# Message sums of a graph layer in turns of 24 steps, with rows fetched by byte offsets into two places

## The reference, cut to what matters

```
h   = relu(x @ w1 + b1)
msg = ew[:, None] * h[src]
agg = segment_sum(msg, dst, num_segments=12500)
z   = agg @ w2 + b2
out = relu(batch_norm(z))        # and a second batch norm behind it
```

## Time and profile before

| what | us |
|---|---|
| median of 3 runs | 5294.92 |
| lowest and highest | 5294.16, 5295.47 |
| the profiled execution's own time | 5292.76 |
| its span, first to last instruction | 5290.7 |
| first gather of layer 1's sum to its last add | 190.86 to 2100.60 |
| first gather of layer 2's sum to its last add | 2260.84 to 4170.76 |

### The profile page before, as it was taken

How to read it: one execution, slowest core, us unless ns; L and a number is a source line. 1 busy time by engine, 2 the same in 40 slices (tenths; PEclk the granted TensorE clock), 3 DMA queues, 4 the chain that set the end, 5 groups by cost and what they waited for, 6 DMA issues and landing times. The chain is left out here.

```text
span 5290.7 us, 129431 instructions
## 1 busy us (share of the span) xinstructions
PE 4201.0 (79%) x20156; PEld 3563.5 (67%) x20157; DVE 3115.8 (59%) x8711; ACT 855.8 (16%) x1985; POOL 3822.4 (72%) x3848
## 2 busy tenths in 40 slices
PE   6778788787787877668777777888778488699998
PEld 5666666666666666556666666666666388599998
DVE  6555555555555555655555555555555665566665
ACT  4200000000000000500000000000000365454444
POOL 2577777777777776677777777777777367678887
PEclk9776767767767676876777777776776555799999
DMA  5433333333333333233333333333333287245554
GB/s 158 131 108 108 108 108 108 108 108 108 108 108 108 108 108 91 91 109 108 109 108 108 108 108 108 108 109 108 108 108 108 67 192 154 48 78 78 79 78 74
DMA packets 360681, 560.51 MB, mean 106 GB/s; under 512 B 128514, under 2 KB 254114, under 8 KB 360483
## 3 DMA queue, kind: packets, MB, share of 16 engines
q0 software_dynamic: 192864, 454.73, 33.0%
q1 hardware_dynamic: 134434, 85.69, 6.7%
q10 hardware_dynamic: 33312, 19.33, 1.4%
HBM read 478.91 MB, written 80.47 MB: 106 GB/s over the span
## 5 line engine op out<-in xcount | busy, mean ns | idle before, releaser
L836 POOL DMA_INDIRECT c_messages<-h,c_indices x3038 | 2880.7, 948 | 950.8 <-issue 919.3
L872 PE MATMUL c_partial<-c_onehot,c_messages 128*128 128x128 f32 x12544 | 2794.3, 375 | 811.8 <-DMA c_messages<-h,c_indices 411.0
L872 PEld LDWEIGHTS c_partial<-c_onehot,c_messages 128*128 128x128 f32 x12544 | 2289.5, 262 | 1319.1 <-issue 767.9
L915 DVE TENSOR_TENSOR sums<-sums,c_partial 128x256 f32 x3136 | 1322.3, 422 | 1591.0 <-PE c_partial L872 1534.4
L888 DVE TENSOR_SCALAR c_onehot<-iota,edge_dst,edge_w 128x128 f32<-128x128 f32 x3152 | 1152.0, 366 | 12.7 <-PEq L113 12.6
L798 ACT ACTIVATE c_indices<-edge_src 128x16 int32 (+1 forms) x200 | 42.9, 215 | 3706.3 <-PE c_partial L872 2914.8
L1804 POOL DMA_INDIRECT out<-ffn_result,ffn_table x210 | 335.0, 1595 | 88.7 <-issue 35.2
L1845 PE MATMUL ffn_ps<-ffn_xT,ffn_w_tile 128*128 128x256 f32 x1680 | 381.9, 381 | 0.0
L1845 PEld LDWEIGHTS ffn_ps<-ffn_xT,ffn_w_tile 128*128 128x128 f32 x1680 | 313.1, 191 | 37.8
L1787 POOL DMA_INDIRECT ffn_rows<-tokens,ffn_table x218 | 239.5, 1099 | 67.9 <-issue 62.2
L852 PE MATMUL c_z<-sums,w 128*128 x768 | 266.1, 510 | 0.0
(11 more groups left out here) (184 smaller groups left out, 2656.2 us busy)
## 6 DMA issues: line engine op xcount, KB each, us to landing
c_messages<-h SPq DMA_DIRECT2D x6272, 1.0 KB
c_messages<-h ACTq DMA_DIRECT2D x6272, 1.0 KB
c_messages<-h,c_indices POOLq DMA_INDIRECT x3038, 2.8
pi_x<-in_x SPq DMA_DIRECT2D x14, 896.0 KB
h<-pi_h ACTq DMA_DIRECT2D x14, 896.0 KB
rt_x<-in_x SPq DMA_DIRECT2D x14, 896.0 KB
out<-rt_x SPq DMA_DIRECT2D x14, 896.0 KB
tokens<-rt_tokens SPq DMA_DIRECT2D x14, 896.0 KB
```

What stands on the lines that cost most here:

```text
L836: pool.indirect_dma_start(messages[:, k, :], None, source, bass.IndirectOffsetOnAxis(ap=indices[:, k:k + 1], axis=0)).then_inc(s_message[k ...
L872: last = pe.matmul(partial[:, k % TURN_BANKS, g * P:(g + 1) * P], messages[:, k, g * P:(g + 1) * P], onehot[:, k % TURN_ONEHOTS, :], start ...
L915: dve.tensor_tensor(where, where, partial[:, k % TURN_BANKS, 0:C].rearrange("p (g n) -> p g n", g=CG), ALU.add).then_inc(s_added, 1)
```

## The change

A turn has 24 steps, not 32. There are 65 full turns and a short one of 3 steps, so all 1563 steps and no empty ones. POOL gathers 23 steps of a full turn and the 3 of the short one. The chunk of nodes per turn is 192, not 256, and there are 65 chunks; the product stands before step 16 and the statistics before step 20.

The fetched step has two slots (`place` 0 and 1), used in turn, so the loops of SP, ACT and PE hold two turns in a round. A turn's rows wait until the turn before the last has been multiplied. The sources are offsets in bytes: `plan_tiles` multiplies the fetched steps' row numbers by 1024 into `row_offset`, and each DMA takes a register as it is for the offset into the source seen as bytes. Registers are loaded 32 at a time, and the next column is fetched behind the second load. ACT no longer copies indices; DVE does, after steps 11 and 22. `add_bias` stands between two fetches of ACT.

```diff
-TURN = 32
+TURN = 24
 FETCHED = TURN - 1
-HALVES = ((0, 16), (16, FETCHED))
+HALVES = ((0, 12), (12, FETCHED))
 TURN_BANKS = 4
 TURN_ONEHOTS = 8
-TURNS = -(-EDGE_TILES // TURN)
+TURNS = EDGE_TILES // TURN
+STEPS_LEFT = EDGE_TILES - TURNS * TURN
-ROW_BATCH = 16
+ROW_BATCH = 32
+ROW_BYTES = C * 4
-Z_COLS = 256
+Z_COLS = 192
-Z_AT = 16
+Z_AT = 12
...
                 dve.tensor_copy(dest[:, c0 * P:c1 * P], turned[:, g % 4, 0:(c1 - c0) * P]).then_inc(s_out, 1)
+                if (a, c1) == (0, K):
+                    dve.wait_ge(s_out, g + 1)
+                    dve.tensor_scalar(t["row_offset"][:], t["edge_src"][:, FETCHED:FETCHED + TURNS * TURN + 1:TURN],
+                                      float(ROW_BYTES), None, ALU.mult)
...
-        messages = sb("messages", [P, TURN, C], F32)
+        messages = sb("messages", [P, TURN + 1, C], F32)
-        s_row = [sem("s_row_sp"), sem("s_row_act")]
+        s_row = [[sem(f"s_row_{e}{u}") for u in range(2)] for e in ("sp", "act")]
+        source_bytes = source.rearrange("(a n) c -> a (n c)", a=1).bitcast(U8)
...
                 eng.dma_start(row_index[0:1, b, :],
-                              t["edge_src"][b * SHARE:(b + 1) * SHARE, bass.ds(turn * TURN + FETCHED, 1)]
+                              t["row_offset"][b * SHARE:(b + 1) * SHARE, bass.ds(turn, 1)]
                               ).then_inc(s_column[b], 16)
-        def fetch_rows(eng, regs, b, turn):
+        def load_offsets(eng, regs, b, batch):
+            eng.load(regs, row_index[0:1, b, batch * ROW_BATCH:(batch + 1) * ROW_BATCH])
+        def fetch_batch(eng, regs, b, batch, place):
+            for n in range(ROW_BATCH):
+                first = bass.RuntimeValue.of_register_unchecked(regs[n]).with_bounds(
+                    min_val=0, max_val=(NODES_PAD - 1) * ROW_BYTES)
+                row = b * SHARE + batch * ROW_BATCH + n
+                eng.dma_start(messages[row:row + 1, FETCHED + place, :].bitcast(U8),
+                              source_bytes[0:1, bass.ds(first, ROW_BYTES)]).then_inc(s_row[b][place], 16)
+        def fetch_rows(eng, regs, b, turn, place):
             gate(eng, s_column[b], turn * 16 + 16, passed)
-            for first in range(0, SHARE, ROW_BATCH):
-                eng.load(regs, row_index[0:1, b, first:first + ROW_BATCH])
-                for n in range(ROW_BATCH):
-                    node = eng.snap(regs[n], min_val=0, max_val=NODES_PAD - 1)
-                    row = b * SHARE + first + n
-                    eng.dma_start(messages[row:row + 1, FETCHED, :], source[bass.ds(node, 1), :]
-                                  ).then_inc(s_row[b], 16)
+            load_offsets(eng, regs, b, 0)
+            if not isinstance(turn, int):
+                gate(eng, s_multiplied, turn * TURN, passed)
+            fetch_batch(eng, regs, b, 0, place)
+            load_offsets(eng, regs, b, 1)
             fetch_column(eng, b, turn + 1)
+            fetch_batch(eng, regs, b, 1, place)
...
             fetch_column(sp, 0, 0)
-            with sp.Fori(0, TURNS) as i:
-                gate(sp, s_multiplied, (i + 1) * TURN, passed)
-                fetch_rows(sp, regs, 0, i)
+            fetch_rows(sp, regs, 0, 0, 0)
+            with sp.Fori(0, TURNS // 2) as i:
+                fetch_rows(sp, regs, 0, i * 2 + 1, 1)
+                fetch_rows(sp, regs, 0, i * 2 + 2, 0)
...
-            turn_of(0, False)
-            with act.Fori(1, TURNS) as i:
-                turn_of(i, True)
+            fetch_rows(act, regs, 1, 0, 0)
+            with act.Fori(0, TURNS // 2) as i:
+                fetch_rows(act, regs, 1, i * 2 + 1, 1)
+                add_bias(i * 2)
+                fetch_rows(act, regs, 1, i * 2 + 2, 0)
+                add_bias(i * 2 + 1)
...
+            pool.wait_ge(s_index, TURNS * 2 + 1)
+            for k in range(STEPS_LEFT):
+                gather(k)
...
+                    slot = FETCHED + place if k == FETCHED else k
...
                         for b in range(2):
-                            pe.wait_ge(s_row[b], i * (16 * SHARE) + 16 * SHARE)
+                            pe.wait_ge(s_row[b][place], round_ * (16 * SHARE) + 16 * SHARE)
...
-            turn_of(0, False)
-            with pe.Fori(1, TURNS) as i:
-                turn_of(i, True)
+            turn_of(0, TURN, False)
+            with pe.Fori(0, TURNS // 2) as i:
+                turn_of(i * 2 + 1, TURN, True, 1, i)
+                turn_of(i * 2 + 2, TURN, True, 0, i + 1)
+            turn_of(TURNS, STEPS_LEFT, False)
...
+            def copy_indices(turn, half):
+                first, end = HALVES[half]
+                dve.tensor_copy(indices[:, first:end], t["edge_src"][:, bass.ds(turn * TURN + first, end - first)]
+                                ).then_inc(s_index, 1)
...
                     build(k % TURN_ONEHOTS, n + TURN_ONEHOTS).then_inc(s_onehot, 1)
+                    for half, (first, end) in enumerate(HALVES):
+                        if k == end - 1:
+                            copy_indices(i + 1, half)
...
+            t["row_offset"] = held("row_offset", [P, TURNS + 1], I32)
```

More of the change, by code:

```diff
@@ L21 @@
 U32 = mybir.dt.uint32
+U8 = mybir.dt.uint8
 P = 128
@@ L785, in _ @@
             fetch_column(sp, 0, 0)
-            with sp.Fori(0, TURNS) as i:
-                gate(sp, s_multiplied, (i + 1) * TURN, passed)
-                fetch_rows(sp, regs, 0, i)
+            fetch_rows(sp, regs, 0, 0, 0)
+            with sp.Fori(0, TURNS // 2) as i:
+                fetch_rows(sp, regs, 0, i * 2 + 1, 1)
+                fetch_rows(sp, regs, 0, i * 2 + 2, 0)
             sp.wait_ge(s_column[0], 16 * (TURNS + 1))
-            sp.wait_ge(s_added, TURN_BANKS + TURNS * TURN)
+            sp.wait_ge(s_added, TURN_BANKS + EDGE_TILES)
         @block.scalar
         def _(act):
-            def copy_indices(turn, first, end):
-                act.activation(indices[:, first:end], t["edge_src"][:, bass.ds(turn * TURN + first, end - first)],
-                               ACT.Copy).then_inc(s_index, 1)
             regs = [act.alloc_register(f"{name}_row{n}") for n in range(ROW_BATCH)]
-            for first, end in HALVES:
-                copy_indices(0, first, end)
             fetch_column(act, 1, 0)
@@ L811, in add_bias @@
                                    bias=t["columns"][:, 0, co:co + 1]).then_inc(s_z_biased, 1)
-            def turn_of(i, with_chunk):
-                gate(act, s_multiplied, (i + 1) * TURN, passed)
-                fetch_rows(act, regs, 1, i)
-                for first, end in HALVES:
-                    gate(act, s_multiplied, (i + 1) * TURN + end, passed)
-                    copy_indices(i + 1, first, end)
-                    if first == 0 and with_chunk:
-                        add_bias(i - 1)
-            turn_of(0, False)
-            with act.Fori(1, TURNS) as i:
-                turn_of(i, True)
+            fetch_rows(act, regs, 1, 0, 0)
[4 more added lines that the diff above has]
+                add_bias(i * 2 + 1)
             act.wait_ge(s_column[1], 16 * (TURNS + 1))
@@ L830, in _, with gather @@
         def _(pool):
+            def gather(k):
+                pool.indirect_dma_start(messages[:, k, :], None, source,
+                                        bass.IndirectOffsetOnAxis(ap=indices[:, k:k + 1], axis=0)
+                                        ).then_inc(s_message[k], 16)
             with pool.Fori(0, TURNS) as i:
@@ L835, in _ @@
                     for k in range(first, end):
-                        pool.indirect_dma_start(messages[:, k, :], None, source,
-                                                bass.IndirectOffsetOnAxis(ap=indices[:, k:k + 1], axis=0)
-                                                ).then_inc(s_message[k], 16)
+                        gather(k)
+            pool.wait_ge(s_index, TURNS * 2 + 1)
+            for k in range(STEPS_LEFT):
+                gather(k)
         @block.tensor
@@ L855, in product_of, with turn_of @@
                 last.then_inc(s_z, 1)
-            def turn_of(i, with_chunk):
-                for k in range(TURN):
+            def turn_of(i, steps, with_chunk, place=0, round_=0):
+                for k in range(steps):
                     n = i * TURN + k
+                    slot = FETCHED + place if k == FETCHED else k
                     if k == Z_PRODUCT and with_chunk:
@@ L917, in turn_of @@
                                       ALU.add).then_inc(s_added, 1)
+                    if steps < TURN:
+                        continue
                     build(k % TURN_ONEHOTS, n + TURN_ONEHOTS).then_inc(s_onehot, 1)
+                    for half, (first, end) in enumerate(HALVES):
+                        if k == end - 1:
+                            copy_indices(i + 1, half)
+            for half in range(len(HALVES)):
+                copy_indices(0, half)
             dve.sem_inc(s_added, TURN_BANKS)
```

20 lines of the change are left out of this document (12 added, 8 removed).

## The result

| | before | after |
|---|---|---|
| median of the runs, us | 5294.54 (5292.66 to 5295.47, 4 runs) | 5229.82 (5226.58 to 5235.25, 4 runs) |
| the profiled execution, us | 5292.76 | 5229.11 |
| its span, us | 5290.7 | 5227.4 |
| TensorE's mean granted clock | 0.744 | 0.766 |

The ratio is 0.9877, with a 95% interval of 0.9866 to 0.9889: faster by 64.7 us. The direction, the engine that sets the pace and the length of a turn came out as written; 12 us of gain were not in the sum. (On some chips the kernel before took about 8250 us; no time measured there is set beside one from the other chips.)

The account below looks back on a forecast made before the run. POOL's gathers were taken to bound the message sums. Gathers -50.2, ends -3.8, aggregation +1.7 and row_offset +0.5 summed to -51.8 us from 5292.76, so 5241.0; with 2.16 for the median, 5243, range 5236 to 5268.

Parts of the forecast that it names:

- the gathers' term: POOL's first to last gather: fewer gathered steps per layer, 25.1 us less per layer, 50.2 in all.
- the ends' term: Last gather to end of each layer's sums: z product seven steps earlier, 1.9 us less per layer, 3.8 in all.
- The pace maker: Message sums: POOL's gathers set the pace, a full turn of 23 gathers taking 28.84 us.
- SP's turn: SP's row fetches, loads and gates: 32.8 us a turn falls to 27.0, 1.8 under POOL's.
- the ceiling: SP's load of 32 registers: at most 3.6 us, from twice 74 ns for each of the added 16; 2.25 taken.
- rival A: SP's or ACT's fetch becomes the bound, through the 32-register load or the loop's way back; up to 5355 or 5393; 12%.
- Rival B: Row fetch: rows keep their register operation (SP's turn 32.4, 5706 us) or byte DMAs are cut up (7305); slower; 7%.
- ACT's chain: ACT's rows, behind add_bias: 27.0 us issuing plus up to 2.8 landing, at most 29.8 against 31.1 available.
- DVE and the aggregation: DVE: index copies and added statistics cost nothing; aggregating 65 chunks, not 49, adds 1.7 us over four times.
- TensorE: PE in the message sums: work stays about 1512 us in 1877, 81% busy.

Follow-up runs that it names:

- the operation put back: Changed kernel with each row's address computed from its node number again by a register operation, instead of byte offsets: 5874.06 us, ratio 1.1095.
- spread padding: Kernel before with the padding's source rows naming many different rows instead of row 0: 5293.42 us against 5293.51, ratio 1.0001.
- the late drain: Kernel before with padding naming many rows, and POOL waiting for the last addition before the barrier's drain: 5302.80 us, ratio 1.0016.
- the run with loads that are not in it: Changed kernel with SP's first 32 offsets loaded three times in the source; the repeats are not in the program: 5230.15 us, ratio 0.988.
- rounds of 295: Changed kernel with SP fetching a column of 64 words eight more times in each turn but the first: 5670.83 us, ratio 1.0710.

## Why the prediction was right, and where it was wrong

The mechanism was right for the turns, and the forecast was still 13 us too high, outside its range. Two steps of the sum carry that: the gathers' term was 5.1 us too small, by its size, and the ends' term 5.9 us too small, by its reason.

**The pace maker: right.** POOL's turn of 28.80 was forecast as 28.84, 2996 gathers as 2996, with "issue" ahead of them.

**SP's turn: right, with its terms off against each other.** A row is 0.318 (10.17 / 32), forecast 0.334: the two gaps that are left in it are 0.032 each, not 0.040. A load of 32 is 2.10, forecast 2.25 from a line through 1 and 16 registers; that is 66 ns a register, and 55 for each of the added 16, below the 74 and 77 seen before, so the ceiling with its steeper slope was far off. The Trainium skill's 200 ns per register (Runtime: NRT & Kernel Launch, "Instruction fetch mechanics"), which that page gives for registers loaded from HBM, is not what these loads from SBUF show, at 16 or at 32; and by it the kernel would have come out at 6080 us, not over 6100. Turn 26.4, forecast 27.0. So rival A did not come near at 274 instructions and two loads; the runs show it is real a little further on: 0.3 us over POOL's turn costs 24 us, and the longer way back 2.4 us each time.

**Rival B** did not occur, and the kernel with the operation put back gave what it priced as far as SP's own work goes (32.35 in the turn without the way back, 32.4 forecast; 33.6 in the mean). Most of the rest of the 5874 against 5706 is the way back that I had kept in rival A alone, the other part the later last addition: the two cases go together, since a row with more instructions makes the longer round.

**ACT's chain: right, with a wrong term.** The last row of a turn lands 4.3 to 4.6 us after its issue, not 2.8, when both queues issue one every 0.318 us. ACT ends its second half at 1026.59 and waits until 1028.72 for the statistics, 2.1 us spare in a turn. The waits name no row as late.

**DVE and the aggregation: right.** A copy is 0.167, POOL's first gather of a turn has 0.30 ahead of it like the others, and 1.916 for 390 words is the 1.482 + 0.434 of the line through two lengths.

**Gathers, -55.3 and not -50.2: the size of a term.** The step "1497 x 1.251 + 65 x 0.07" charged the difference between the mean pitch and a typical gather to the turn's boundary, and so added 16 boundaries a layer, 1.1 us. The mean pitch was there to be used: 1497 x 1.25323 = 1876.1, 1.2 us nearer in each layer. The other 1.1 and 1.5 are a pitch that fell to 1.2525 and 1.2522. The kernel before with byte offsets alone has the same 1.2522 and 1.2525, so the smaller pitch is there without turns of 24; why, no run shows. Its size is near what two executions differ by: the changed kernel a second time had 1.2528 in both layers.

**The ends, -9.65 and not -3.8: a wrong step.** "The last add of layer 1 starts 7.34 us after the last gather (2100.60 - 2093.26), because the last turn's z product put PE behind. With it seven steps earlier relative to the end I take 5.5". Three things in it fail.

The z product does not come earlier against the end. Before, it stands 12 steps ahead of the end of the last turn; after, it stands 8 steps ahead of the end of the last full turn, and 3 more steps follow, so 11. In the traces it starts 9.7 us before the last gather (2083.53) and 8.7 (2057.49).

The last addition moved all the same, to 4.12 and 4.29 behind the last gather, from 7.34 and 7.49. Spreading the padding alone moved it to 5.03 and 4.72. So most of the move is the empty steps, whose gathers landed 2 us late, and the changed kernel has none; the rest was not taken apart.

And the additions were not what the barrier waited for before: POOL was, in a drain of 23.7 us that the page's busy times don't count, though the wait ahead of PE's next product was named after PE's sequencer, the barrier's own line. The runs with spread padding and with the late drain show that for the kernel before. In the changed kernel both arrive within 0.13 us of each other, and when the same program ran again (the run with loads that are not in it) SP, which waits for the last addition, came 0.12 us behind the drain in layer 1 and 0.13 before it in layer 2. So the 9.65 needed both. With the shorter drain alone, the others would still have come at 8.07 and 8.22: 3.4 us in all. With the earlier additions alone, nothing. That the drain fell from 8.9 to 4.0 us could not be read from any row, and its cause stays open.

**TensorE.** I had its busy time stay at 1512 us in 1877. It fell to 1354, with 112 matmuls more, and the granted clock rose from 0.71 to 0.74. It changes nothing in the time, since PE waits for POOL either way. Byte offsets alone already bring the clock to 0.74 and PE's busy time to 1402 in the kernel before, so that part comes with them; by what way, no run shows.

## What to carry to other kernels

When work is moved from a pace maker to engines with slack, the slack must be found for three things and not one: for issuing, for landing (a second place, 137 us here), and for the loop's own way back once the round grows. Price a phase's end by whatever reaches the barrier last, and list every engine's arrival there, the sequencers' drains among them: a gain at one of them ends where the next one stands. For a long row of equal steps use the measured mean pitch, with what it holds, and not a model of where its excess lies. Ask on how many chips the pace maker was seen: on some, POOL waited for ACT, and the byte offsets alone, worth nothing here, gained 9% there.

## What the runs showed that I had not expected

- The barrier's drain on POOL behind indirect gathers takes 8.9 us in one kernel and about 4 in the other (3.6 on an idle POOL), and on an idle POOL 0.08 us more for each gather more. A second drain right after it takes 0.12 (at 2103.30 in the kernel before).
- Gathers whose 128 indices name one row land 4.7 us after they start, with many rows 2.7. It cost the kernel before nothing, since POOL's drain ended later still.
- Rows of 1 KB issued by two queues at one per 0.318 us each fall behind: in a batch of 32 the first starts to move 1.19 us after its issue, the last 2.05; at one per 0.414 us it stays near 1.1.
- A loop's way back costs a sequencer 0.25 us, or 2.6 in a round of 402 and in one of two rounds of 295; the same 295 instructions had 0.26 in layer 1 and 2.63 in layer 2.
- Rows fetched with one register operation less each raised TensorE's mean granted clock from 0.747 to 0.767 (medians of 21 and 10 executions), with the same matmuls in the same time.
